# Deformable convolution and mixture of experts on one Trainium2 core: sampling the normalised tokens before the projection, and hats of two images by a selection matrix

## The reference, cut to what matters

```
xn  = layernorm over channels(x)
om  = conv3x3(xn, w_off) + b_off            # 27 maps: 9 dy, 9 dx, 9 masks
ys, xs = pixel + tap + (dy, dx);  mask = sigmoid(...)
sampled[c,k,p] = mask[k,p] * bilinear(xn[c], ys[k,p], xs[k,p])   # zero outside
x   = x + einsum('ckp,ock->op', sampled, w_dcn)
t   = tokens(x)
out = t + sum over the 2 best of 8 experts e of
          weight_e * (gelu(layernorm(t) @ W1[e] + b1[e]) @ W2[e] + b2[e])
```

## Time and profile before

| | |
|---|---|
| times of three runs | 97.18, 96.42, 97.77 us (median 97.18) |
| profiled execution: span | 95.2 us |
| the profiled execution's own time | not given apart; the median lies 1.98 us above the span |
| PE / DVE / ACT / POOL busy | 85.9 / 67.5 / 45.1 / 22.9 us |
| DMA | 10.02 MB, of which 18 spread transfers of 384 KB |

### The profile page before, as it was taken

One profiled execution on the slowest core, in us unless ns is written; L12 is line 12 of the kernel. 1 busy time (PEld: TensorE's weight loads), 2 busy tenths in 40 slices (PEclk: granted clock), 3 DMA queues, 4 the chain that ended last, 5 costly groups with the idle time before them and its releaser, 6 DMA issues.

```text
span 95.2 us, 1718 instructions
## 1 busy us (share of the span) xinstructions
PE 85.9 (90%) x574; PEld 46.9 (49%) x574; DVE 67.5 (71%) x185; ACT 45.1 (47%) x88; POOL 22.9 (24%) x33
## 2 busy tenths in 40 slices
PE   3986899899888998989999899999899999999980
PEld 3973356559545974556463544344342332223550
DVE  5695999898899997895955965957936820069550
ACT  5113575969050632341275765418462769652200
POOL 5204000000000072997200002002553150005630
DMA  1719600000419999983999994000000000000003
GB/s 47 213 30 284 267 0 3 0 7 0 121 36 274 262 253 260 260 271 112 249 257 253 251 260 123 0 0 0 3 7 0 0 0 0 0 0 0 0 7 103
DMA packets 5303, 10.02 MB, mean 105 GB/s; under 512 B 1344, under 2 KB 2400, under 8 KB 5296
## 3 DMA queue, kind: packets, MB, share of 16 engines
q1 hardware_dynamic: 4960, 9.54, 37.5%
q0 software_dynamic: 192, 0.30, 1.0%
q10 hardware_dynamic: 144, 0.10, 0.3%
HBM read 9.08 MB, written 0.85 MB: 104 GB/s over the span
## 4 chain that ended last, share of the span: by engine, by line
PE 34%; DMA 21%; DVE 17%; issue 14%; POOL 6%; SPq 3%; POOLq 1%; ACT 1%; DVEq 0%; ACTq 0%
DMA spread_hats<-hat_rows 10%; DMA hat_rows<-hrow_last 8%; PE taps_ps L791 6%; PE bank_o L882 6%; PE hid_ps L869 6%; POOL rs L326 4%; PE bank_o L817 3%; PE taps_ps L869 3%; DMA xt<-in_x_tok 2%; PE bank_c L760 2%; DVE xn L619 2%; PE bank_y L882 2%; SPq L312 2%; DVE a_sb L547 2%; DVE at L535 2%
## 5 line engine op out<-in xcount | busy, mean ns | idle before, releaser
L817 PE MATMUL bank_o<-a_sb,v_sb 128*64 128x256 f32 x144 | 18.0, 386 | 1.0 <-ACT a_sb L412 0.5
L454 ACT ACTIVATE hid<-hid_ps,b_col 128x512 f32<-128x512 f32 x18 | 11.5, 683 | 10.2 <-PE hid_ps L869 10.1
L817 PEld LDWEIGHTS bank_o<-a_sb,v_sb 128*64 128x64 f32 x144 | 9.7, 136 | 8.3 <-issue 2.3
L547 DVE TENSOR_TENSOR a_sb<-spread_hats 128x1536 f32<-128x1536 f32 x6 | 10.9, 1834 | 2.9 <-DMA spread_hats<-hat_rows 2.9
L791 PE MATMUL taps_ps<-ident,at 128*128 128x128 f32 x72 | 11.0, 280 | 1.5 <-DVE a_sb L669 0.8
L326 POOL TENSOR_TENSOR rs<-ve,power 128x2 f32<-128x2 f32 (+1 forms) x6 | 4.8, 806 | 25.7 <-DVE ve L562 21.5
L412 ACT ACTIVATE a_sb<-taps_ps 128x512 f32<-128x512 f32 x11 | 6.4, 597 | 9.2 <-PE taps_ps L791 9.2
L869 PE MATMUL hid_ps<-x2s,w_sb 64*128 64x512 f32 x36 | 10.2, 641 | 0.0
L791 PEld LDWEIGHTS taps_ps<-ident,at 128*128 128x128 f32 x72 | 7.9, 141 | 4.6 <-DVE a_sb L669 3.3
L882 PE MATMUL bank_o<-hid,w_sb 128*64 128x512 f32 x40 | 9.7, 605 | 0.0
L454 ACT ACTIVATE hid<-taps_ps,b_col 128x512 f32<-128x512 f32 x14 | 8.8, 686 | 1.5 <-PE taps_ps L869 1.5
(11 more groups left out here) (133 smaller groups left out, 121.3 us busy)
## 6 DMA issues: line engine op xcount, KB each, us to landing
spread_hats<-hat_rows SPq DMA_DIRECT2D x18, 384.0 KB, 8.1
w_sb<-in_w SPq DMA_DIRECT2D x2, 512.0 KB, 3.9
wdcn<-in_w_dcn SPq DMA_DIRECT2D x2, 144.0 KB, 3.0
xc<-in_x_ch SPq DMA_DIRECT2D x1, 256.0 KB, 4.5
hat_rows<-hrow SPq DMA_DIRECT2D x2, 128.0 KB
hat_rows<-hrow POOLq DMA_DIRECT2D x2, 128.0 KB, 8.1
xt<-in_x_tok SPq DMA_DIRECT2D x1, 192.0 KB, 2.4
out<-xc SPq DMA_DIRECT2D x1, 128.0 KB, 1.7
```

Of the source, the lines that this page charges most:

```text
L454: act.activation(hid[:, m % H_RING, half, c, :], two_banks(f"H{h}.{j}.{c}")[:, half * 512:(half + 1) * 512], ACT.Gelu, bias=b1_col[:, col: ...
L547: dve.tensor_tensor(a_sb[:, slot % A_RING:slot % A_RING + GROUP, :, :], spread_hats[:, 1:, k0:k0 + GROUP, :].rearrange("p s k t -> p k s t ...
L817: last = pe.matmul(bank_o[st * O:(st + 1) * O, 0:HW], v_sb[:, img, st, k, :], a_sb[:, slot % A_RING, st, :], start=(k == 0), stop=(k == TA ...
```

## The change

- **Sampling first.** `M` now multiplies the normalised tokens `xn` (tokens on the partitions) with a, chunk by chunk of two taps (the fifth has one), each chunk in a bank of its own; `se` copies it out with a factor 0.5 (`smp`), and `C` projects with w_dcn, two taps stacked on 128 rows. `V`, `vs`, `xfl`, `osv` and `v_sb` are gone. `xr` adds the projected samples to `xc`; `oT` transposes that, and `st` and `lna` read the bank of `oT`.
- **Hats of images 2 and 3 row by row.** The saved maps have their bias added (`om_sp`) and three rows of pixel positions and ones below; `R.0` and `R.1` multiply them with selection matrices (`pick`), which gives ys - y in rows (k, y) and tokens along the free axis at once. `ay`, `tm`, `al`, `tl` (ACT) take absolute value and tanh, `hr.0` to `hr.2` (DVE) the hats. omT, pos, dist, abs, relu, haty and hT of these images are gone. The constants come from GpSimd (`rows0`) and DVE (`make_constants`), and SP moves them into place by seven small DMAs.
- **Spreading.** `spread_hats` has a place for each of the two images, transfers are by chunks of two taps (30 of them), image 3's don't wait for products, and the product is made in place. `tmp` and `hid` share memory with buffers of the front.
- **Orders and banks.** All four orders are new; all eight banks are given out one by one (`HOMES`) or in pairs (`PAIR_HOMES`). `make_sums` is replaced by a comparison, the full memset of `xpad` by three of its border, `ya0.0` and `ya1.0` are gone.

The core of the diff:

```diff
+PE_ORDER = (
+    "xnT0 early4 conv0 xnT2 omT0 conv2 xnT1 xnT3 R2.0 R2.1 conv1 conv3 omT1 T0.5 R3.0 T0.0 T0.1 T0.4 R3.1 T0.3 T0.2 M0.0 M0.2 "
+    "T0.6 T0.7 T1.1 T1.0 T0.8 M0.3 M0.1 M0.4 M1.0 T1.3 T1.2 T1.6 T1.4 T1.7 T1.5 T1.8 M1.1 M1.2 M1.3 C0.0 M1.4 C0.1 C1.0 oT0 C1.1 "
+    "M2.1 oT1 M2.2 M2.3 M2.4 xT0 xT1 M2.0 gate0 H0.1.0 H0.1.1 H0.2.0 H0.0.1 H0.2.1 wdT0 M3.0 M3.1 M3.2 M3.3 O0.2 C2.0 M3.4 C3.0 "
+    "C2.1 C3.1 sp0.1 sp0.0 H0.0.0 oT2 oT3 O0.1 O0.0 xT3 xT2 H0.3.1 gate1 H1.1.0 H1.0.0 H0.3.0 H1.2.0 H1.0.1 H1.1.1 wdT1 O0.3 O1.0 "
+    "sp1.0 sp1.1 H1.3.1 H1.2.1 H1.3.0 O1.1 O1.2 F0 O1.3.1 O1.3.0 Fa1.1 Fa1.0 F1.1 F1.0 "
+DVE_ORDER = (
+    "stats0 stats1 xn0 xpu0 xn2 xn1 xn3 xpu2 base0 pos0 dist0 xpu1 xpu3 relu0 haty0 hr2.0 pr0.2.0 pr0.2.1 pr0.0.1 hr2.1 pr0.0.0 "
+    "pos1 hr2.2 pr0.1.0 pr0.1.1 dist1 pr0.3.1 pr0.3.0 relu1 haty1 pr1.0.0 pr1.0.1 pr0.4.1 pr0.4.0 E0.2 hr3.0 pr1.3.1 E1.0 pr1.1.0 "
+    "pr1.1.1 pr1.2.1 pr1.3.0 hr3.2 pr1.2.0 pr1.4.1 pr1.4.0 hr3.1 pd2.0 E1.4 E1.8 se1.0 pd2.1 pd2.2 pd2.3 xr0 se1.4 pd2.4 xr1 st0 "
+    "st1 lna0 lna1 pd3.0 pd3.1 top0 se2.3 idx0 wd0 pd3.2 pd3.3 pd3.4 se3.3 se3.4 xr3 xr2 st3 st2 lna3 lna2 tmp0.0 tmp0.2 tmp0.1 "
+POOL_ORDER = (
+    "rstd0 rows0 rstd1 sel0 dw3 rstdt0 rstdt1 rstdt3 rstdt2 ya0.1 ya0.2 ya0.3 ya1.1 ya1.2 "
...
+            sp.wait_ge(pool_rows, 6)
+            sp.wait_ge(pick_ready, 1)
+            for r in range(3):
+                row = slice(POS_ROW + r, POS_ROW + r + 1)
+                sp.dma_start(om_sp[row, :, :], crow[:, r * HW:(r + 1) * HW].unsqueeze(1).broadcast_to([1, len(SPREAD), HW])).then_inc(ld_pos, 16)
...
+                for q in range(CHUNKS):
+                    sp.dma_start(spread_hats[:, i, 0, taps, :], flat[1].unsqueeze(1).broadcast_to(shape)).then_inc(there, 16)
...
+                elif kind == "R":
+                    pe.wait_ge(ld_pos, 16 * 7)
+                    pe.wait_ge(*saved(om_saved, f"om{b}"))
+                    if n[1] == 0:
+                        for c in range(2):
+                            last = pe.matmul(bank(step)[:, c * HW:(c + 1) * HW], pick[c], om_sp[:, i, :], start=True, stop=True)
+                    else:
+                        pe.matmul(bank(step)[:, 0:HW], pick[2], om_sp[:, i, :], start=True, stop=True)
+                        last = pe.matmul(bank(step)[0:3 * W, HW:2 * HW], pick_last, om_sp[:, i, :], start=True, stop=True)
...
+                elif kind == "M":
+                    for st in range(ST):
+                        for place, k in enumerate(taps):
+                            col = place if len(taps) == 2 else st
+                            last = pe.matmul(bank(step)[col * C:(col + 1) * C, 0:HW], xn[:, NT * b + st, 0, :], tap(b, k, st),
+                                             start=(st == 0 or len(taps) == 1), stop=(st == ST - 1 or len(taps) == 1))
...
+                elif kind == "C":
+                    for q in chunks:
+                        for j in range(NT):
+                            last = pe.matmul(bank(f"C{b}.0")[j * O:(j + 1) * O, 0:P], wdcn[:, q, :], smp[:, b, q, j * P:(j + 1) * P],
+                                             start=(q == 0), stop=(q == CHUNKS - 1))
...
+            def make_rows():
+                places = crow[:, 0:2 * HW].rearrange("p (c y x) -> p c y x", c=2, y=H)
+                for c, pattern in enumerate(([[1, H], [0, W]], [[0, H], [1, W]])):
+                    pool.iota(places[:, c, :, :], pattern=pattern, base=0, channel_multiplier=0,
+                              allow_small_or_imprecise_dtypes=True).then_inc(pool_rows, 1)
+                pool.memset(crow[:, 2 * HW:3 * HW], 1.0).then_inc(pool_rows, 1)
```

More of the change, by code:

```diff
@@ L92 @@
[L92 to L107, removed]
+HOMES = (
+    (
+        "xnT0 conv0 omT0 R2.1 T0.5 M0.2 T1.1 T1.6 M3.1 C3.0 O0.0 wdT1 O1.0 "
+    ),
+    (
+        "xnT2 conv2 R2.0 conv1 omT1 T0.1 T0.3 T1.0 T1.2 T1.5 O0.3 O1.1 Fa1.0 "
+    ),
+    (
+        "xnT1 T0.0 M0.0 M1.0 oT0 M2.0 O0.2 "
+    ),
+    (
+        "xnT3 conv3 R3.0 T0.6 T0.8 M0.1 M1.1 C1.0 oT1 xT1 C2.0 oT2 xT3 "
+    ),
+    (
+        "T0.4 T0.2 M0.3 M0.4 M1.2 C0.0 M2.2 wdT0 M3.3 oT3 xT2 F0 "
+    ),
+    (
+        "R3.1 T1.3 T1.8 M1.3 M1.4 M2.1 xT0 M3.0 M3.2 M3.4 O0.1 O1.3.1 Fa1.1 "
+    ),
+    (
+        "T0.7 T1.4 M2.4 O1.2 O1.3.0 "
+    ),
+    (
+        "T1.7 M2.3 "
+    ),
+)
@@ L110, in kind_of @@
+PAIR_HOMES = (
+    (
+        "H0.1.0 H0.0.0 gate1 H0.3.0 "
+    ),
+    (
+        "H0.1.1 H0.2.1 H1.1.0 H1.0.1 H1.3.1 "
+    ),
+    (
+        "gate0 H0.2.0 sp0.1 H1.0.0 H1.1.1 sp1.1 H1.3.0 "
+    ),
+    (
+        "H0.0.1 sp0.0 H0.3.1 H1.2.0 sp1.0 H1.2.1 "
+    ),
+)
+BANK = {step: home for home, steps in enumerate(HOMES) for step in steps.split()}
+PAIR = {step: home for home, steps in enumerate(PAIR_HOMES) for step in steps.split()}
 def kind_of(step):
@@ L117, in numbers, with engine_of, upto, chunk_taps @@
     return [int(n) for n in step[len(kind_of(step)):].split(".")]
+def engine_of(step):
+    return next(n for n, order in ORDERS.items() if step in order)
+def upto(*steps):
+    order = ORDERS[engine_of(steps[0])]
+    last = max(order.index(step) for step in steps)
+    return sum(kind_of(s) == kind_of(steps[0]) for s in order[:last + 1])
+def chunk_taps(q):
+    return range(2 * q, min(2 * q + 2, TAPS))
 def metaformer_kernel(nc, x_tok, x_ch, w_off, b_off, w_dcn, wg, bg, w1, b1, w2, b2, out):
@@ L531, in product @@
+            def product(b, q, j):
+                i = DIRECT.index(b)
+                u = CHUNKS * i + q
+                k0, m = chunk_taps(q)[0], len(chunk_taps(q))
                 dve.wait_ge(haty_ready, upto(f"haty{b}"))
                 if u >= AT_RING:
-                    dve.wait_ge(tap_T, GROUP * (u - AT_RING + 1))
-                shape = [P, GROUP, H, W]
+                    before, chunk = divmod(u - AT_RING, CHUNKS)
+                    dve.wait_ge(tap_T, upto(*(f"T{DIRECT[before]}.{k}" for k in chunk_taps(chunk))))
+                shape = [P, m, H, W]
@@ L710, in _ @@
+                    dve.tensor_tensor(xc[:, b, part], home[:, part], xc[:, b, part], ALU.add).then_inc(fin_ready, 1)
         @block.tensor
         def _(pe):
-            released = {}
-            def take(name, *waits):
-                for sem_, value in released.get(name, ()):
-                    pe.wait_ge(sem_, value)
-                released[name] = waits
-            def keep_warm(n, bank):
-                for _ in range(n):
-                    pe.matmul(bank[:, 0:P], ident[:, :], ident[:, :], start=True, stop=True)
@@ L735, in _, with take_two, keep_warm, tap @@
+            def take_two(step, *waits):
+                take((2 * PAIR[step], 2 * PAIR[step] + 1), *waits)
+            def keep_warm(n, home):
+                for _ in range(n):
+                    pe.matmul(home[:, 0:P], ident[:, :], ident[:, :], start=True, stop=True)
+            def tap(b, k, st):
+                if b in SPREAD:
+                    return spread_hats[:, SPREAD.index(b), 1 + st, k, :]
+                return a_sb[:, k, st, :]
             pe.wait_ge(pool_const, 2)
-            keep_warm(WARM, bank_y)
+            keep_warm(WARM, banks[3][:, 512:])
@@ L820, in _ @@
                 elif kind == "oT":
-                    take(BANK[step], (var2, upto(f"st{b}")))
-                    pe.wait_ge(fold_ready, 1)
-                    pe.wait_ge(*saved(o_saved, f"osv{b}"))
+                    h, i = divmod(b, 2)
+                    part = slice(i * C, (i + 1) * C)
+                    take_bank(step, (xn2_ready, upto(f"lna{b}")))
+                    pe.wait_ge(xr_ready, upto(f"xr{b}"))
                     for j in range(NT):
-                        last = pe.matmul(misc(step)[:, j * O:(j + 1) * O], o_sb[:, b, j * P:(j + 1) * P], fold[:, :], start=True, stop=True)
+                        last = pe.transpose(bank(step)[:, j * C:(j + 1) * C], xc[part, h, j * P:(j + 1) * P], ident[part, part])
@@ L881, in _ @@
                         for half in range(2):
-                            last = pe.matmul(part(y_bank(step)[O * half:O * half + O, :]), w2_sb[:, j + PAIRS * half, c, :],
+                            last = pe.matmul(part(bank(step)[O * half:O * half + O, :]), w2_sb[:, j + PAIRS * half, c, :],
                                              part(hid[:, (PAIRS * h + j) % H_RING, half, c, :]), start=(c == 0), stop=(c == HC - 1))
```

675 lines of the change are left out of this document (326 added, 349 removed), and 19 rows, old and new, of tables (ACT_ORDER, DVE_ORDER, PE_ORDER).

## The result

The changed kernel takes 91.41 us (median of four runs, 91.20 to 92.19) beside 97.17 for the kernel before in the same session: ratio 0.942 with the interval 0.935 to 0.950. The profiled execution took 91.2 us with a span of 89.3 (95.2 before). The forecast was 96.0 with a range from 93.0; the result lies 4.6 us under the one and 1.6 under the other. Some executions of either kernel take 1.5 to 3% longer than its others without any edit; the medians and ratios in this document leave them out.

The account below looks back on a forecast made before the run. TensorE was taken to bound the end, TensorE and VectorE both nearly full in the middle, latency before 15.4. Span 95.2 less 1.05 of net TensorE work gave 94.1; plus 1.98 made 96.1, given as 96.0, range 93.0 to 99.5.

Parts of the forecast that it names:

- The end: TensorE from gate0 at 46.9: 39.65 us of steps plus 1.5 idle, O1.2 ending at 88.1 instead of 89.15.
- the sum of 30.6: VectorE's in-order work from haty0 to lna1, 30.6 us, so lna1 ends at 45.6 and gate0 starts at 46.9.
- TensorE sets the end: From 47.6 on in the kernel before, TensorE was taken as the limit: 39.5 of 41.6 us listed as work.
- The start: Up to haty0: ends at 15.0 instead of 13.69, +1.3 us, with the seven DMAs hidden by 0.5.
- The 16.6 us taken for image 3's transfers: From first issue to last product as before, putting image 3's last chunk at 53.6, with no wait of weight.
- The late list of 39.65: TensorE's steps from gate0 to the end of O1.2, priced from the earlier trace at 39.65 us.
- The idle time of 1.5: TensorE's waits after gate0: 2.1 us as before, 0.5 by a walk of all queues, 1.5 taken.
- Rival 1: TensorE orders mesh better: late idle 0.5, middle idle a microsecond less; time 94.1, chance 0.32.
- Rival 2: Latency, not TensorE, is the bound: image 3's last product 5.6 us sooner passes on; time 91.6, chance 0.06.
- worth only what idle time it removes: An earlier image 3 gains only TensorE idle time, since TensorE had other work while its data landed.
- Rival 3: GpSimd's row building slower, delaying VectorE and R2.0: 97.6 at 2.7 ns an element, 99.5 to 100 at 4; chance 0.12.
- Rival 4: ScalarE in the last third: eight H in a row outpace its gelus; up to 1.2 us, 97.2, chance 0.08.

Follow-up runs that it names:

- run 14: Changed kernel with five expert steps moved on TensorE so that H and O alternate more, no step added: 97.9 us, ratio 1.006 to the kernel before.
- run 1: Changed kernel with wait-free TensorE steps appended behind its last result: six H and six O take 15.80 us in runs, 17.56 alternating.
- run 11: Kernel before with O0.3 put directly behind O0.2, ahead of H1.0.0: 98.2 us, ratio 1.010.
- run 3: Changed kernel with pd3.0 and pd3.1 behind wd0, and image 3's spread transfers held until st1 is done: 97.4 us, ratio 0.997 to the kernel before.
- run 6: Changed kernel with gelus in TensorE's H order and all H, gate0 and sp on two pairs of banks instead of four: 103.4 us, ratio 1.065.
- run 13: Kernel before, orders untouched, image 3's transfers reading image 2's rows so they need not wait for their own: 96.87 us, ratio 0.994.
- run 4: Changed kernel with pd3.0 and pd3.1 behind wd0, and GpSimd's rows0 iotas and memset issued twice: 94.21 us, ratio 0.966 to the kernel before.
- run 5: Changed kernel with ScalarE's gelus in the order of TensorE's H steps, H1.2.0 two places later: 92.6 us, ratio 0.959 to the kernel before.
- run 12: Kernel before with image 3's transfers reading image 2's rows and product pd8 moved ahead of st1: 98.9 us, ratio 1.020.

## Why the prediction was wrong

The step that failed is "The end": a list of 39.65 us at the prices of the earlier trace rows with 1.5 us of idle time on top. The runs show 37.85 with next to none. A second, smaller one is the sum of 30.6 for VectorE in the middle, which came to 28.1.

The forecast span was 94.1, the measured one 89.3. The 4.8 us are three parts of its own sum: gate0 starts at 45.2 where I had 46.9 (-1.7), the late stretch takes 37.85 where I had 39.65 and 1.5 idle (-3.3), the tail is 6.25 instead of 6.05 (+0.2).

**What held.** TensorE sets the end. The start: rows0 1.8 us (1.7 said), haty0 at 15.52 (15.0, within 14.1 to 16.1), R2.0 from 12.58 to 13.52 (13.9), so that SP's seven DMAs stayed hidden. R costs 2.0 an image (1.9 said), V, hT and xfl are gone. No spread transfer is waited for; the last product, at 51.6, is even 2 to 3 us ahead of the forecast. The 16.6 us taken for image 3's transfers held a wait for the products of image 2 that is gone (15.0 at most now, 36.59 to 51.6). The tail is as said but for 0.2.

**The middle, VectorE's sum of 30.6.** It is 28.1 (15.52 to lna1's end at 43.6). I added durations, or durations less 0.03; here the instructions start closer than that. A product of 512 elements takes 0.60 from start to start, not the 0.66 taken (16 of them: 1.0 us), and the four E 0.60 each instead of 0.69 (0.4). The hr cost 2.6, as said. From st0 to the end of lna1 it is 3.1 us where I had 3.8: the 0.9 of waiting for rstd is 0.1. haty0's half microsecond went the other way. The middle idle of TensorE that I forecast, 3.5 us, shrank with it to 1.0 (26.82 busy of the 27.81 from the first T at 17.31 to gate0).

**The late list of 39.65.** H 15.0 instead of 15.4, O 12.5 instead of 13.1, M3 3.96 instead of 4.35, sp 1.4 instead of 1.8, oT2 and oT3 0.2 instead of 0.45, while xT, the gates and C are 0.35 more: 37.85. The prices came from single places of a list in which the kinds alternate, and even there they did not fit: start to start, the sixteen H of the kernel before take about 16.3 us and not 15.4 (0.96 in a pair of H, 1.06 for one ahead of an O), and its seven O 12.9. The same steps take 15.0 and 12.5 now, 1.7 less. What the list missed of H stood in the prediction as idle time: the 2.1 us of the kernel before were 1.0 (40.47 busy of 41.45).

Counting from the order lists, TensorE changes the kind of step 87 times before and 54 times after, from the first gate or H to F0 33 times before and 21 times after; if only changes between shapes of array use count (64 rows by 128 columns for H, 128 by 64 for O, M and C, 128 by 128 for T), it is 29 before and 13 after. Sixteen changes at 0.10 to 0.18 (runs 14 and 1) are 1.6 to 2.9 us, and the list is 1.8 shorter than I had it. The Trainium skill (TensorEngine Tiling (Array Packing), Key Properties) says that a change of the tiling mode drains TensorE; it gives no price. The starts of runs 1 and 14 agree, with 0.10 to 0.18 us for one. I had costed "all orders anew" on TensorE at nothing. That the whole 1.8 is this is an inference from the price and the count: in run 11 a wait took what the pair saved, and run 14 was drowned by waits.

**The idle time of 1.5.** I had found 0.5 by walking the queues, and put 1.0 on top for small waits. It is 0.03 in one profiled execution and 0.16 of the 38.43 in the other. Runs 3, 6 and 14 show what it rests on: image 3's data by 50 (late by 5.0: +5.5 us), the banks as they were given out (two pairs: +11, with the first H badly placed), and this very order (five steps moved: +6).

**The rivals.** Rival 1, orders that mesh better, was right in kind: both of its gains came, and it was still 2.7 us too slow, as it kept my prices. Rival 2's 91.6 lies within 0.2 us of the measured time, and yet its mechanism is not what happened: in the kernel before, 1.5 us of earlier data passed on half of themselves (run 13), and after, TensorE is busy without a gap. What run 3 adds is that early landing is needed for the new order, not a gain by itself; "worth only what idle time it removes" held for the kernel before and left out that a new order would be built on it. The Trainium skill (Perfetto Trace Analysis, Identifying the Most-Contended Engine) has the busy share of weight loads as one of two measures of headroom. It reads 46% in the late stretch (17.36 of 37.85), in which TensorE never stood still: taken as the time that this list could still give up, it misleads here. Rival 3's path is real (run 4), its price did not arise: iotas of 256 and 384 elements cost 1.5 to 1.6 ns an element, those of 144 2.2, not 2.7 or 4. Rival 4 did not arise: the seven H from H0.3.1 to H1.1.1 (I had counted eight) run without a wait.

**What stays open.** Sampling before projecting without the new orders was not built, so how much of the gain is the algebra (about 1 us by the sum of removed and added steps) and how much the order is worked out, not measured. The price of 2 KB against 3 KB runs is open too, and so is what four bank pairs alone are worth.

## What to carry to other kernels

Price a step from a run of equal steps and add the changes of kind apart: on TensorE 0.10 to 0.18 us each here, on VectorE use start to start. When a change rewrites all orders, count waits and kind changes of the new lists instead of keeping the old idle time, and expect the result to have no slack: moving a few steps by hand cost 1 to 6 us in runs 5, 11, 12 and 14, mostly because one in-order instruction then stood before its data or its bank's reader. The gain to be had was found the same way, by asking which instruction is queued ahead of the one that TensorE waits for (top0 behind pd3.1, together with a lighter VectorE: 0.9 to 1.4 us).
